# First head group's maxima rows, ones rows, two chunks of keys and first values made ready within the first pass over the context

## The chip, the cores and the metric

The kernel runs on one core of a Trainium2 chip as one program, in one launch. The metric is the time of one execution on the device, in microseconds (us). The profile adds the trace of one execution. Engines: TensorE (PE in the rows, its weight loads PEld), VectorE (DVE), ScalarE (ACT), GpSimd (POOL), and SyncE (SP), which issues the DMA transfers.

## The reference

A layer of a perceiver on 512 latents of 512 channels, with a context of 8192 rows. Only the first of its three parts is touched:

```python
def _L0_xattn_ref(query_modal, key_value_modal, Wq, bq, Wk, bk, Wv, bv, Wo, bo):
    q = _split_heads(query_modal @ Wq.T + bq)      # 16 heads of 32
    k = _split_heads(key_value_modal @ Wk.T + bk)
    v = _split_heads(key_value_modal @ Wv.T + bv)
    scores = jnp.einsum('bhnd,bhmd->bhnm', q, k) * scale
    attn = jax.nn.softmax(scores, axis=-1)
    x = jnp.einsum('bhnm,bhmd->bhnd', attn, v)
    ...
    return x @ Wo.T + bo

x = x + _L0_xattn_ref(_layernorm(x, axis=-1), ctx_1024, ...)
x = x + _L0_attn_ref(_layernorm(x, axis=-1), ...)   # self attention, then a sparse mixing over heads
x = x + _L0_ffn_ref(_layernorm(x, axis=-1), ...)    # 8 experts, top 2
```

## The kernel before

The program is a row of blocks. Each block holds a hand-written instruction list for every engine, ordered by semaphores, and no engine enters the next block before all have finished the one at hand.

**Preparation** (`prepare`, L113) makes the queries, and the keys of the first of 16 context chunks (512 rows each).

**First pass** (`project_context`, L278). It projects all chunks to keys and values and stores them in DRAM, since they don't fit in the on-chip memory, and finds for each query row and head the maximum score. `ITEMS` lists 32 projections (16 chunks for keys, 16 for values), each of four parts, numbered by `o`. GpSimd splits each chunk into a rounded high part (cast, L98) and the low rest (subtraction, L100), `split_chunk`. The maxima come from pairs of chunks: max(a, b) = (a + b)/2 + |a - b|/2, so keys are added and subtracted pairwise (`k_sum`, `k_dif`: on VectorE for the first pair, L502 and L503, on GpSimd later, L392 and L393). 256 steps (`STEPS`) follow, 32 for a pair of chunks (block `m`), eight for a head group `g` of four heads. In step `i` TensorE makes the difference scores of step i + 1 (`dif`, L430), once ScalarE has read those of step i (`s_size`, L445), the sum scores of step i (`tot`, two banks), and four or six matmuls of the projections (L86), into two banks `proj`. ScalarE takes the magnitude of the difference (L481) and evacuates finished projections (L470, L474). VectorE adds and takes the running maximum (L519). It may lag: TensorE's step i waits for the maxima of step i - 2 (L447). In the last block of chunks head group 0 is through at step 231, and `row_maxima` (L505) reduces the maxima of three head groups at step 248 and those of the last at the end.

SyncE stores keys and values (`store_keys`, L371). Behind the parts of the third-last and second-last items it also copies the queries into the tile `stacks` (`queries`, L356, twelve transfers a half). At the block's end it waits for all stores and copies (L376 to L381). TensorE ends with eight warm-up matmuls (`keep_warm`, L275).

**Second pass** (`attend_context`, L543). For each of four head groups it runs over all 16 chunks in tiles of 128 context rows, 64 tiles a group, numbered by `T`. Keys lie in one of three buffers `kst` with 98 rows: high keys, low keys, high keys again, and two rows of ones; values in one of three buffers `val`. One score matmul (L700) multiplies these with the tile `stacks`, whose 96 rows of queries are followed by two rows that hold the negated maximum, high and low part; so the scores come out shifted and ScalarE takes the exponential straight away (L801) into `pr`. TensorE weights the values (L714), VectorE adds up the exponentials (L851).

Before the first score matmul of this block, VectorE clears a tile and puts the negated maxima into it (L828 to L825), TensorE runs sixteen warm-up matmuls, transposes the tile (`turn`, L604), warms up again, ScalarE and VectorE copy the four rows into `stacks` (`take_row`, L610), GpSimd writes the ones rows of the three key buffers (L627, L631), ScalarE loads its table with a one-element exponential (L790), and SyncE loads keys (L656) and values (L661) of the first three chunks.

Of the kernel before, what the change touches and what calls it, by code (L numbers as in the profile page):

```python
# [20 lines left out]
P = 128  # L21
D = 512
# [255 lines left out]
def project_context(nc, c):  # L278
# [35 lines left out]
    with ExitStack() as stack:  # L314
# [12 lines left out]
        best = sb("best", [P, H * NT, BLOCKS])  # L327
        dif = pb("dif", [P, 2 * CH])
# [5 lines left out]
        v_out = [sem(f"v_out{w}") for w in range(2)]  # L334
        nc.clear_and_free_semaphores(c.spent)
        c.spent = used
        block = stack.enter_context(nc.Block())

# [6 lines left out]
        def _(sp):  # L345
# [12 lines left out]

            for o in range(4 * len(ITEMS)):
# [16 lines left out]
            for w in range(2):  # L376
                sp.wait_ge(k_hi_out[0][w], 16 * (NCH // 2))
                sp.wait_ge(k_hi_out[1][w], 16 * (NCH // 2))
                sp.wait_ge(k_lo_out[w], 16 * NCH)
                sp.wait_ge(v_out[w], 16 * NCH)  # L380
            sp.wait_ge(s_stack, 16 * 2 * 3 * HG)  # L381

        @block.gpsimd
        def _(pool):
# [9 lines left out]

            for i in range(2, len(ITEMS)):
                if i % 4 == 2 and i > 2:
                    pairs(i // 4)
                split_chunk(pool, c, i)

        @block.tensor  # L400
        def _(pe):
            def project(o, begin, end):
                kind, n = ITEMS[o // 4]
                b, at, out = o // 4 % RING, o % 4, proj[o % 2][:, :]
                if begin == 0:
                    if at == 0:
                        pe.wait_ge(c.s_lo, o // 4 + 1)

                    if kinds[o - 2] == "k":
# [27 lines left out]
            for i in range(STEPS):  # L437
# [13 lines left out]
                for piece in pieces(i):  # L451
                    project(*piece)
            pe.wait_ge(s_size, STEPS)
# [3 lines left out]
        def _(act):  # L457
# [19 lines left out]
            for i in range(STEPS):  # L477
# [4 lines left out]
                for o in finished(i):  # L482
                    evacuate(o)

        @block.vector
        def _(dve):
# [22 lines left out]

            LAST = STEPS - 2 * NT  # L510
            first_pair(0)
            low(FIRST - 1)
            for i in range(STEPS):
# [8 lines left out]
                for o in finished(i):  # L522
                    low(o)
                if i == LAST:
                    row_maxima(slice(0, HG * (G - 1)), LAST)
            row_maxima(slice(HG * (G - 1), H), STEPS)
            dve.wait_ge(s_best, 2)
# [15 lines left out]
def attend_context(nc, c):  # L543
# [26 lines left out]
    with ExitStack() as stack:  # L570
        sb, pb, sem = allocators(nc, stack, "att")
        kst = [sb(f"kst{b}", [STK + 2, HG, CH], F32R) for b in range(CHUNKS)]
        val = [sb(f"val{b}", [P, KT, P]) for b in range(CHUNKS)]
# [5 lines left out]
        k_in = [sem(f"k_in{b}") for b in range(CHUNKS)]  # L579
        v_in = [sem(f"v_in{b}") for b in range(CHUNKS)]  # L580
# [3 lines left out]
        s_row = [sem(f"row{half}") for half in range(2)]  # L584
# [25 lines left out]
        def take_row(engine, h, bank, done):  # L610

            j = h % HG
            src, dst = bank[HD * j:HD * j + 2, 0:N], c.stacks[MROW:MROW + 2, h, :]
            if engine.engine == mybir.EngineType.Activation:
                engine.activation(dst, src, ACT.Copy).then_inc(done, 1)
            else:
                engine.tensor_copy(dst, src).then_inc(done, 1)
# [1583 lines left out]
```

## Time and profile before

| | us |
|---|---|
| median of 3 runs | 1576.19 |
| lowest and highest run | 1572.24, 1576.27 |
| the profiled execution's time | 1577.37 |
| its span, first to last instruction | 1575.7 |

| engine | busy in the span |
|---|---|
| TensorE matmuls | 1506.9 us, 96% |
| VectorE | 1240.7 us, 79% |
| ScalarE | 1022.8 us, 65% |
| GpSimd | 410.5 us, 26% |

The busy share is a mean over stages with different limits, and it counts warm-up matmuls as work. Times within the trace run from the start of the span. The first pass lasts from about 47 to 570 us, the second from there to about 1140.

### The profile page before, as it was taken

Reading aid. Unit: us, or ns where it says so; the run is one execution under the profiler, and the core shown is the slowest. Engines: PE = TensorE matmul, PEld = TensorE weight load, DVE = VectorE, ACT = ScalarE, POOL = GpSimd, SP = SyncE. Lnnn points to the kernel's source line nnn. Section 1 sums busy time; section 2 is a strip of 40 time slices with the busy share of each in tenths; the row PEclk is TensorE's granted clock in tenths of the full one; section 3 lists DMA queues with packets and bytes.
Section 4 is the critical chain, followed back from the end, with each engine's and each line's share of the span. In section 5 each row is a group of like instructions: output and inputs, shape, how many; then the busy total and the mean of one; then the engine's idle time right before and its main releaser. Section 6 shows DMA issues by size and latency. Waiting matters only on the chain. (4 is left out here: it accounts for less than half of the span.)

```text
span 1575.7 us, 23638 instructions
## 1 busy us (share of the span) xinstructions
PE 1506.9 (96%) x8658; PEld 871.1 (55%) x8658; DVE 1240.7 (79%) x1876; ACT 1022.8 (65%) x1343; POOL 410.5 (26%) x225
## 2 busy tenths in 40 slices
PE   6899999999999999999999999999999955999998
PEld 4566666666666554444444444444345732799995
DVE  6777776776767769999998999999876878476664
ACT  3366666666666768888888888888737941244441
POOL 5554546545456010501200400100004420200002
PEclk9899999999999999999999999999999987899999
DMA  6354443544435365446645454445237045399994
GB/s 236 111 200 147 162 176 127 191 148 173 174 132 189 104 164 125 124 127 174 175 114 153 115 128 114 128 114 130 59 54 161 2 178 205 127 340 348 362 331 141
DMA packets 119778, 254.59 MB, mean 162 GB/s; under 512 B 10152, under 2 KB 26536, under 8 KB 115184
## 3 DMA queue, kind: packets, MB, share of 16 engines
q1 hardware_dynamic: 117632, 248.35, 50.6%
q0 software_dynamic: 1408, 4.46, 0.9%
q8 instruction: 70, 1.15, 0.3%
q10 hardware_dynamic: 624, 0.27, 0.1%
q14 instruction: 44, 0.36, 0.1%
HBM read 182.26 MB, written 61.34 MB: 155 GB/s over the span
## 5 line engine op out<-in xcount | busy, mean ns | idle before, releaser
L801 ACT ACTIVATE att_pr<-b_sc 128x1024 f32<-128x1024 f32 x512 | 482.2, 1035 | 74.8 <-PE b_sc L700 73.4
L851 DVE TENSOR_TENSOR att_tot<-att_tot,att_pr 128x2048 f32<-128x2048 f32 x184 | 430.2, 2338 | 21.4 <-ACT att_pr L801 3.3
L519 DVE CUSTOM_DVE_ANT_0 ctx_size<-ctx_tot,ctx_size 128x512 f32<-128x512 f32 x512 | 333.1, 689 | 130.5 <-PE ctx_tot L430 127.1
L481 ACT ACTIVATE ctx_size<-ctx_dif 128x1024 f32<-128x1024 f32 x256 | 262.4, 1025 | 122.6 <-PE ctx_dif L430 122.5
L700 PE MATMUL b_sc<-g_stacks,att_kst 98*128 98x512 f32 x1024 | 293.3, 418 | 2.0 <-DMA att_kst<-keys_scratch 1.5
L700 PEld LDWEIGHTS b_sc<-g_stacks,att_kst 98*128 98x128 f32 x1024 | 175.0, 188 | 186.1 <-ACT att_pr L801 136.2
L714 PE MATMUL b_o<-att_pr,att_val 128*32 128x512 f32 x2048 | 255.4, 600 | 0.9 <-issue 0.9
L430 PE MATMUL ctx_dif<-ctx_k_dif,f_q_hi 32*128 32x512 f32 x512 | 127.9, 497 | 7.3 <-DVE ctx_best L519 6.0
L430 PE MATMUL ctx_tot<-ctx_k_sum,f_q_hi 32*128 32x512 f32 x512 | 128.5, 499 | 0.0
L86 PE MATMUL f_proj<-g_stacks,f_wk_hi 128*128 128x512 f32 x352 | 120.4, 423 | 0.7 <-DVE f_k_lo L211 0.7
L86 PE MATMUL f_proj<-f_wv_hi,g_stacks 128*128 128x512 f32 x320 | 120.7, 421 | 0.0
L714 PEld LDWEIGHTS b_o<-att_pr,att_val 128*32 128x32 f32 x2048 | 48.8, 108 | 114.9 <-issue 95.2
L1907 PEld LDWEIGHTS ex_hp<-ex_xT,m_w 128*128 128x128 f32 x960 | 109.3, 192 | 3.0 <-issue 1.8
L1907 PE MATMUL ex_hp<-ex_xT,m_w 128*128 128x128 f32 x960 | 109.8, 275 | 0.8 <-issue 0.8
L430 PEld LDWEIGHTS ctx_dif<-ctx_k_dif,f_q_hi 32*128 32x128 f32 x512 | 47.6, 182 | 103.9 <-issue 52.4
L100 POOL TENSOR_TENSOR g_stacks<-f_raw,g_stacks 128x2048 fp32r<-128x2048 f32 x21 | 97.2, 4630 | 1.7
L1966 ACT ACTIVATE g_stacks<-m_w 128x1024 fp32r<-128x1024 f32 x56 | 54.6, 1047 | 63.9 <-PE ex_yp L86 63.9
L851 DVE TENSOR_TENSOR att_tot<-att_pr 128x2048 f32<-128x2048 f32 x36 | 84.1, 2335 | 13.0 <-ACT att_pr L801 13.0
L621 POOL TENSOR_TENSOR o_aoT<-att_whole,att_rs 128x512 f32<-128x512 f32 x3 | 9.4, 3141 | 324.2 <-DVE att_rs L858 324.2
L86 PEld LDWEIGHTS f_proj<-g_stacks,f_wk_hi 128*128 128x128 f32 x352 | 60.8, 191 | 30.0 <-issue 20.4
L86 PEld LDWEIGHTS f_proj<-f_wv_hi,g_stacks 128*128 128x128 f32 x320 | 59.6, 188 | 29.2 <-issue 18.3
L86 PE MATMUL f_proj<-f_wv_hi,f_third 128*128 128x512 f32 x192 | 72.4, 421 | 0.0
(314 smaller groups left out, 2182.2 us busy)
## 6 DMA issues: line engine op xcount, KB each, us to landing
m_w<-in_W SPq DMA_DIRECT2D x30, 2048.0 KB, 10.3
att_kst<-keys_scratch SPq DMA_DIRECT2D x192, 256.0 KB, 3.9
f_raw<-in_ctx SPq DMA_DIRECT2D x32, 1024.0 KB, 5.9
keys_scratch<-f_k_hi SPq DMA_DIRECT2D x32, 512.0 KB, 2.8
keys_scratch<-f_k_lo SPq DMA_DIRECT2D x32, 512.0 KB, 3.1
values_scratch<-ctx_v SPq DMA_DIRECT2D x32, 512.0 KB, 3.2
att_val<-values_scratch SPq DMA_DIRECT2D x64, 256.0 KB, 2.6
rows_scratch<-mix_blank SPq DMA_DIRECT2D x1, 3840.0 KB, 23.8
```

Of the source, the lines that this page charges most:

```text
L86: mm = pe.matmul(out, left, right, start=(n == 0), stop=(n == 3 * len(a) - 1))
L100: pool.tensor_tensor(c.lo[b], raw[:, :, :], f32(c.hi[b]), ALU.subtract).then_inc(c.s_lo, 1)
L430: mm = pe.matmul(out[:, r * CH:(r + 1) * CH], c.q_hi[rows, g, t * P:(t + 1) * P], keys[m % 2][rows, g, :], start=True, stop=True)
L481: act.activation(size[:, i % ABS, :], dif[:, :], ACT.Abs).then_inc(s_size, 1)
L519: dve.tensor_tensor_reduce(out=size[:, i % ABS, r * CH:(r + 1) * CH], in0=tot[i % 2][:, r * CH:(r + 1) * CH], in1=size[:, i % ABS, r * CH: ...
L621: engine.tensor_tensor(c.aoT[:, g, :], whole[:, :], rs[:, :], ALU.mult).then_inc(s_norm, 1)
L700: mm = pe.matmul(sc[pair % PAIRS][:, r * N:(r + 1) * N], kst[m % CHUNKS][:, j, at:at + P], c.stacks[0:STK + 2, HG * (T // PER_G) + j, :], ...
L714: mm = pe.matmul(o[at, :], val[m % CHUNKS][:, T % KT, at], pr[:, T % SLOTS, j, :], start=first, stop=False, skip_group_check=True)
L801: act.activation(pr[:, T % SLOTS, 2 * s:2 * s + 2, :], sc[(2 * T + s) % PAIRS][:, :].rearrange("p (j q) -> p j q", j=2), ACT.Exp, scale=SC ...
L851: dve.tensor_tensor(tot[b % 2][:, :, :], so_far, pr[:, T % SLOTS, :, :], ALU.add).then_inc(s_add, 1)
L1907: mm = pe.matmul(hp[tau % 2][:, f, :], w1[b][:, k, f * P:(f + 1) * P], xT[tau % 2][:, k, :], start=(k == 0), stop=(k == DC - 1))
L1966: act.activation(w2_hi[:, fs, :], w2[tau % 2][:, fs, :], ACT.Copy).then_inc(s_hid, 1)
```

## The change

Work that stood at the start of the second pass is done within the first, for head group 0 alone:

- Buffers: two of the key buffers `kst` and one of the value buffers are now allocated for both passes. They lie where the two buffers of raw context chunks (`raw`) lie, and later stages get their tiles at that place too (`same_place`).
- GpSimd clears a tile `first` at the start of the first pass, and at its end writes the ones rows of two key buffers.
- VectorE reduces the maxima of head group 0 at step `EARLY` = 232, and puts them into `first` at the next step (`first_shifts`).
- TensorE transposes `first` into a free bank `proj` at step `TURN` = 249, behind the matmuls of that step. Part 127, the last, uses the bank next and waits for the four row copies. ScalarE makes one copy in step 250 and two in step 251, VectorE one in step 251 (`take_row`).
- SyncE issues the keys of two chunks and the values of one (`first_keys`) right behind the query copies, ahead of the last two stores of values. The block's end waits for these loads and no longer for the last values: ScalarE and VectorE wait for those in the second pass, at its second tile and its start.
- ScalarE's one-element exponential stands at the end of the first pass.
- The second pass starts with the score matmuls. The warm-ups, the transposes and row copies ahead of them are gone.

```diff
+            def first_keys():
+                for w in range(2):
...
+                    sp.wait_ge(v_out[w], 16)
+                for b in range(2):
+                    sp.wait_ge(c.s_lo, len(ITEMS) - 1 + b)
+                    for row, part in ((0, 0), (1, 1), (2, 0)):
+                        sp.dma_start(f32(c.kst[b][HD * row:HD * row + HD, :, :]),
+                                     c.k_dram[b, 0, part].rearrange("(j d) k -> d j k", j=HG)).then_inc(c.k_first[b], 16)
+                sp.dma_start(c.val[:, :, :], c.v_dram[0, 0]).then_inc(c.v_first, 16)
...
                     queries(o // 4 - (len(ITEMS) - RING))
-            for w in range(2):
-                sp.wait_ge(k_hi_out[0][w], 16 * (NCH // 2))
...
-                sp.wait_ge(v_out[w], 16 * NCH)
+                    if o // 4 == len(ITEMS) - 2:
+                        first_keys()
             sp.wait_ge(s_stack, 16 * 2 * 3 * HG)
+            for b in range(2):
+                sp.wait_ge(c.k_first[b], 48)
+            sp.wait_ge(c.v_first, 16)
...
+            pool.memset(first[:, :, :], 0.0).then_inc(s_blank, 1)
             for i in range(2, len(ITEMS)):
...
+            for b in range(2):
+                pool.memset(f32(c.kst[b][MROW:MROW + 2, :, :]), 1.0).then_inc(s_ones, 1)
...
+                    if o == LATE + 2:
+                        pe.wait_ge(s_row, HG)
...
+                if i == TURN:
+                    pe.wait_ge(v_done, count("v", LATE + 1))
+                    pe.wait_ge(s_shift, 3)
+                    for tile in range(NT):
+                        mm = pe.transpose(turned[:, tile * P:(tile + 1) * P], first[:, tile, :], c.ident[:, :])
...
+                if i == TURN + 1:
+                    take_row(act, 0)
+                if i == TURN + 2:
+                    take_row(act, 1)
+                    take_row(act, 2)
+            act.activation(once[:, :], c.ones[:, 0:1], ACT.Exp).then_inc(s_once, 1)
...
+            def first_shifts():
+                parts = first[:, :, :].rearrange("p t (j w) -> p j t w", w=HD)
+                dve.wait_ge(s_best, 1)
+                dve.tensor_scalar(first_hi[:, :, :], c.neg[:, 0:HG, :], -1.0, None, ALU.mult).then_inc(s_shift, 1)
...
+                if i == EARLY:
+                    row_maxima(slice(0, HG), EARLY)
+                if i == EARLY + 1:
+                    first_shifts()
+                if i == TURN + 2:
+                    take_row(dve, HG - 1)
...
-            keep_warm(pe, den[:, 0:P], c.ident[:, :], c.ident[:, :], 16)
-            pe.wait_ge(s_shift, 4)
-            turn(pe, sc[0])
-            keep_warm(pe, den[:, 0:P], c.ident[:, :], c.ident[:, :], 4)
-            pe.wait_ge(s_ones, 1)
-            for half in range(2):
-                pe.wait_ge(s_row[half], HG // 2)
...
-            act.activation(std[:, 0:1], c.ones[:, 0:1], ACT.Exp).then_inc(s_early, 1)
-            act.wait_ge(s_turned, 1)
-            for h in range(1, HG, 2):
-                take_row(act, h, sc[0], s_row[1])
             for T in range(TILES):
...
+                elif T == 1:
+                    for w in range(2):
+                        act.wait_ge(c.v_out[w], 16 * NCH)
...
-            shifts(0)
-            dve.wait_ge(s_turned, 1)
-            for h in range(0, HG, 2):
-                take_row(dve, h, sc[0], s_row[0])
+            for w in range(2):
+                dve.wait_ge(c.v_out[w], 16 * NCH)
```

## Rows read from the trace of the kernel before

**Rows 1.** Busy us of each engine by stretch; then granted clock, DMA share, GB/s.

```profile
700.00:800.00 100.00, 100.00 (x608) 42.61 (x610) 95.59 (x45) 86.29 (x93) 16.84 (x6) 1.00 0.62 165
```

**Rows 2.** Groups of TensorE in the second pass: busy, mean ns | idle before, releasers.

```profile
L700 PE MATMUL b_sc<-g_stacks,att_kst 98*128 98x512 f32 x1024 | 293.3, 418 | 2.0 <-DMA att_kst<-keys_scratch 1.5 <-ACT att_pr L801 0.5
```

**Rows 3.** Timeline between the passes: start us, duration us, engine, line [idle before <-releaser].

```profile
566.59 2.14 PE L275 MATMUL ctx_dif<-f_wv_hi 128*128 128x512 f32 x8
...
568.16 0.29 DVE L507 TENSOR_REDUCE g_neg<-ctx_best 128x16 f32<-128x128 f32 x1
570.42 1.80 POOL L627 MEMSET att_kst<- 2x2048 f32 x1 [54.99 <-POOLq L314]
570.42 1.28 ACT L790 ACT_TABLE_LOAD   x1 [3.56 <-PEq L314]
570.42 1.28 SPq L656 DMA_DIRECT2D att_kst<-keys_scratch  x3
...
570.46 3.81 PE L275 MATMUL b_den<-g_ident 128*128 128x128 f32 x32 [1.73 <-PEq L314]
...
571.00 1.27 DVE L829 TENSOR_SCALAR att_shift_hi<-g_neg 128x64 fp32r<-128x64 f32 x1
...
572.30 0.18 DVE L824 COPY o_yT<-att_shift_hi 128x16 f32<-128x16 f32 x1
...
574.10 0.60 PE L607 MATMUL b_sc<-g_ident,o_yT 128*128 128x128 f32 x4
...
574.74 1.20 ACT L615 ACTIVATE g_stacks<-b_sc 2x512 fp32r<-2x512 f32 x2 [2.82 <-PE b_sc L607]
...
577.08 1.63 PE L700 MATMUL b_sc<-g_stacks,att_kst 98*128 98x512 f32 x6 [1.49 <-DMA att_kst<-keys_scratch]
```

**Rows 4.** SyncE's waits in 540 to 600 us: total, times, longest.

```profile
SPq L380 <- DMA values_scratch<-ctx_v: 2.4, 1, 2.4
```

**Rows 5.** Stretches by engine as in rows 1, opening and boundary.

```profile
60.00:62.00 2.00, 2.00 (x9) 1.07 (x8) 2.00 (x6) 0.25 (x1) 1.72 (x1) 0.50 0.00 0
74.00:78.00 4.00, 4.00 (x15) 2.29 (x12) 2.47 (x7) 1.77 (x3) 0.00 (x0) 0.50 0.02 4
560.00:562.00 2.00, 2.00 (x13) 1.07 (x10) 1.44 (x6) 1.62 (x3) 0.00 (x0) 1.00 0.00 0
572.00:574.00 2.00, 2.00 (x21) 2.00 (x20) 0.53 (x3) 0.00 (x0) 0.21 (x1) 1.00 0.99 246
```

**Rows 6.** Timeline of the first pass's opening.

```profile
47.05 0.70 PE L86 MATMUL f_proj<-f_third,f_wk_hi 128*128 128x512 f32 x2 [0.30 <-PEq L117]
47.32 2.18 POOL L98 CAST g_stacks<-f_raw 128x2048 fp32r<-128x2048 f32 x1 [15.14 <-POOLq L117]
...
47.66 2.38 DVE L503 TENSOR_TENSOR ctx_k_sum<-f_k_hi 128x512 fp32r<-128x512 f32 x1
...
58.69 0.50 PE L430 MATMUL ctx_dif<-ctx_k_dif,f_q_hi 32*128 32x512 f32 x2 [2.84 <-DVE ctx_best L519]
...
62.20 0.68 DVE L503 TENSOR_TENSOR ctx_k_sum<-f_k_hi 128x512 fp32r<-128x512 f32 x1
...
66.81 4.74 DVE L502 TENSOR_TENSOR ctx_k_dif<-f_k_hi 128x512 fp32r<-128x512 f32 x1
```

**Rows 7.** Timeline of SyncE's issues near the first pass's end.

```profile
554.01 2.52 SPq L356 DMA_DIRECT2D g_stacks<-g_hT  x4
557.16 10.10 SPq L371 DMA_DIRECT2D values_scratch<-ctx_v  x2
```

**Rows 8.** Timeline of the first pass's last steps.

```profile
556.79 0.55 DVE L507 TENSOR_REDUCE g_neg<-ctx_best 128x48 f32<-128x384 f32 x1
...
558.12 0.18 PEld L430 LDWEIGHTS ctx_dif<-ctx_k_dif,f_q_hi 32*128 32x128 f32 x2 [0.42 <-ACT ctx_size L481]
...
558.66 1.03 ACT L481 ACTIVATE ctx_size<-ctx_dif 128x1024 f32<-128x1024 f32 x1 [0.60 <-PE ctx_dif L430]
558.81 0.69 DVE L519 CUSTOM_DVE_ANT_0 ctx_size<-ctx_tot,ctx_size 128x512 f32<-128x512 f32 x1 [0.25 <-PE ctx_tot L430]
```

More of the change, by code:

```diff
@@ L333, in project_context @@
         k_hi_out, k_lo_out, s_pair0 = c.k_hi_out, c.k_lo_out, sem("pair0")
-        v_out = [sem(f"v_out{w}") for w in range(2)]
+        v_out = c.v_out = [sem(f"v_out{w}") for w in range(2)]
+        c.k_first, c.v_first = [sem(f"k_first{b}") for b in range(2)], sem("v_first")
+        s_ones, s_blank, s_shift, s_turned, s_row, s_once = (
+            sem(n) for n in ("ones", "blank", "shift", "turned", "row", "once"))
         nc.clear_and_free_semaphores(c.spent)
@@ L583, in attend_context @@
         s_rs, s_norm, s_out = sem("rs"), sem("norm"), sem("out")
-        s_row = [sem(f"row{half}") for half in range(2)]
+        s_row = sem("row")
         shift_hi = sb("shift_hi", [P, H, NT], F32R)
@@ L612, in take_row @@
             j = h % HG
[L613 to L617, printed above, removed]
+            engine.tensor_copy(c.stacks[MROW:MROW + 2, h, :], bank[HD * j:HD * j + 2, 0:N]).then_inc(done, 1)
         def weigh(engine, g):
@@ L654, in _ @@
                     sp.wait_ge(s_sc, 2 * KT * (m - CHUNKS + 1))
-                for row, part in ((0, 0), (1, 1), (2, 0)):
+                for row, part in ((0, 0), (1, 1), (2, 0)) if m >= len(c.kst) else ():
                     sp.dma_start(f32(kst[b][HD * row:HD * row + HD, :, :]),
@@ L977, in self_projections @@
         rstd = sb("rstd", [P, 2, H])
[L978 removed]
+        cen = c.cen
         sq = sb("sq", [P, D])
@@ L2096, in perceiver_layer, with same_place @@
         c.stacks = sb("stacks", [P, H, N], F32R)
+        def same_place(*shapes):
+            with ExitStack() as room:
+                sb, _, _ = allocators(nc, room, "k")
+                return [sb(name, shape, dt) for name, shape, dt in shapes]
+        c.raw = same_place(*((f"raw{b}", [P, DC, CH], F32) for b in range(2)))
+        (c.cen,) = same_place(("cen", [P, 3, D], F32))
+        c.held, c.wide, c.room = same_place(*((n, [P, 2, N], F32) for n in ("held", "wide", "room")))
+        c.z, c.left, c.zs = same_place(*((n, [P, 2, N], F32) for n in ("z", "left", "zs")))
+        c.hid_hi, c.hid_lo = ([tile[:, FC * b:FC * b + FC, :] for b in range(2)] for tile in same_place(
+            *((n, [P, 2 * FC, P], F32R) for n in ("hid_hi", "hid_lo"))))
+        c.kst = [sb(f"kst{b}", [P, HG, CH], F32R) for b in range(2)]
+        c.val = sb("val", [P, KT, P])
         with ExitStack() as first:
```

93 lines of the change are left out of this document (57 added, 36 removed).

## The prediction

> **What bounds the kernel now.** I read the busy time by stretch first. In 700 to 800 us, inside the second pass over the context, TensorE is busy all 100 us at full granted clock, VectorE 95.6, ScalarE 86.3 [rows 1]. The list of groups for the whole second pass says the same: before all 1024 score matmuls TensorE sat idle 2.0 us, of which 1.5 us waited for a key load [rows 2]. So the pass cannot be shortened by this change, but it can start earlier, and what is taken off before its first score matmul moves everything behind it by as much, because no stage between there and the end starts by an outside event.
>
> Then I read the timeline between the passes [rows 3]. The last work of the first pass is TensorE's eight warm-up matmuls, ended by 566.59 + 2.14 = 568.73, and VectorE's last maximum, ended by 568.45. All engines set off again only near 570.4. Then: shifts on VectorE, four transposes on TensorE at 574.10, row copies from 574.74, and the first score matmul at 577.08, released by a key load that was issued at 570.42. From 568.73 to 577.08 are 8.35 us in which TensorE does nothing that the result needs, save the transposes. The list of the queue's waits names what held the block's end: SyncE waited 2.4 us for the last store of values [rows 4]. Key loads of the second pass cannot be issued sooner, as they stand behind that end. In 572 to 574 us the DMA engines are 0.99 busy, in 560 to 562 they move nothing [rows 5].
>
> **What is removed.** Before the first scores: the warm-up and transposes on TensorE (3.81 + 0.60 us and another small warm-up), the table load (1.28), the row copies (1.20 for ScalarE's two), the first wait for keys, and SyncE's 2.4 us wait, since the block's end no longer asks for the last values. What then ends the first pass is TensorE's warm-up and VectorE's maximum. At the boundary before, from preparation to first pass, where no store was awaited, TensorE sat idle 0.30 us [rows 6]. So without any added cost the first score matmul would start at 568.73 + 0.30 = 569.03, which is 8.05 us earlier.
>
> **What is added, and where it shows.**
>
> *The blank tile's memset, on GpSimd at the start of the first pass.* GpSimd's memset of 2048 elements per partition took 1.80 us [rows 3]; 512 elements make some 0.45 us by that row. There GpSimd is on the path: its cast and subtraction of a chunk share time with VectorE's sums of the first keys. A sum took 2.38 us while the cast ran and 0.68 us when it didn't, and TensorE then waited 2.84 us for VectorE [rows 6]. So I count the whole 0.45 us. From below it is 0 (something else later); from above 0.45 + 0.68 = 1.13, if a sum of VectorE also gets in ahead of the delayed cast.
>
> Of this the Trainium skill (SBUF — State Buffer, "Who interferes with whom") says that a VectorE instruction with two SBUF inputs is held by a GpSimd instruction that reads SBUF, not by one that only writes it, and that whichever starts first holds the other. The cast and the 2.38 us agree. By that rule the memset would not hold the sum at 47.66, which would run before the cast; the cast would end 0.7 us later, the subtraction behind it would be spared the sum that now delays it by 0.3, and the cost would be 0.4 instead of 0.45.
>
> *Seven loads of 256 KB on SyncE's queue (six of keys, one of values), ahead of the last two stores of values.* SyncE issues the second half of the query copies until 556.5, then stands waiting; its next store was issued at 557.16 [rows 7]. Seven issues at 0.43 us (three took 1.28 [rows 3]) are 3.0 us, so that store moves to about 559.6, and nobody waits for it until the second tile of the second pass. The data is 1.84 MB, with the store 2.36 MB; at the 246 GB/s of 572 to 574 [rows 5] this takes 9.6 us from 556.5, so it lands near 566, in a stretch that is now empty. The block's end at about 570 waits for it, so the cover is some 4 us; it is gone when the rate falls under 172 GB/s (2.36 MB in 13.7 us). I take 0. The last store has landed today when the block ends, near 570.4, and with 1.5 us of later work (below) near 571.9. ScalarE's second tile, which now waits for it, comes behind two exponentials, each as large as the magnitude that took 1.03 us [rows 8], so not before 570.5 + 2.06 = 572.6. So 0 again, with 0.7 us to spare.
>
> *The ones rows on GpSimd (two of 1.80 us).* They follow its last chunk split; GpSimd was idle 54.99 us before the second pass [rows 3]. 0.
>
> *First maxima, and three small operations on VectorE, some 23 steps before the end.* A step lasts 1.03 + 0.60 = 1.63 us, ScalarE's magnitude and its wait; VectorE sits idle 0.25 in it [rows 8]. A reduction three times as long as the new one took 0.55 and did no harm. Small operations took 0.18; 1.27 is the longest such row, beside a running GpSimd memset [rows 3]. TensorE's step waits for the maxima of two steps before, so a short lag of VectorE reaches nobody. I take 0; from above 0.8 us, if one lasts 1.27.
>
> *Four transposes on TensorE, three row copies on ScalarE, one on VectorE, in the last seven steps.* This is the term that counts. ScalarE and TensorE hand each step to one another: ScalarE is free 0.60 us of a step, TensorE 0.42 [rows 8]. Transposes took 0.60 [rows 3], so the next step's difference starts some 0.2 late. The first copy (0.60) waits for them and starts late by as much again: ScalarE's next magnitude is 0.45 later than now. The two other copies stand in one step: 1.20 us in a gap of 0.60, so 0.60 more. Together 1.05. From below 0.6 (only the second of the pair shows), from above 1.8 (three copies with no gap at all). VectorE's copy ends 0.69 + 2 × 0.69 + 0.60 = 2.67 us into its step (start of its maxima, the two, a copy as long as ScalarE's), TensorE wants it for the last projection after 1.63 + 0.60 = 2.23: 0.44 late, which the 0.42 us gap swallows. I take 0, from above 0.45.
>
> *The exponential's table on ScalarE at the end.* 1.28 us and one tiny operation, 0.2 at most, behind the last values. ScalarE has ended today 3.56 us before 570.42 [rows 3]; with 1.5 us of later work and this it ends at 569.85, TensorE's warm-up at 570.23. 0, with only 0.4 us of cover.
>
> The remaining edits only give tiles other places, or move shifts within VectorE, which has nothing to add until two exponentials are done. 0.
>
> **Sum.** First scores at 569.03 + 0.45 + 1.05 = 570.53 instead of 577.08: 6.55 us gained. With all lower costs 569.63 (7.45 gained), with all upper ones 569.03 + 1.13 + 0.8 + 1.8 + 0.45 = 573.21 (3.87 gained). The profiled execution took 1577.37 for a span of 1575.7, so the span becomes 1569.2 and that execution 1570.8. It lies 1.2 us above the median of the runs, 1576.19; from that median the forecast is 1569.6.
>
> **Rivals.**
>
> *The boundary still waits for a transfer (8%).* The loads go out behind twelve query copies, and today's first key load took 6.6 us to release TensorE, sharing the engines with the other loads [rows 3, 5]. For: that figure. Against: the empty stretch. If they land at 572.5 to 575 the gain is 2 to 4.5 us, 1571.7 to 1574.2. TensorE would then idle longer; in 60 to 62 us, after its 2.84 us wait, its granted clock was 0.50, that is 1.2 GHz instead of 2.4, while the idle 1.73 us at today's boundary left it at 1.00 [rows 3, 5, 6].
>
> Beside this stands the Trainium skill (TensorE: Matmul & The Clock Gate, "Part 1"): idleness of the array throttles its clock to half, sustained work restores it. The trace agrees at 60 to 62 us. The warm-ups that the change takes out would matter by that rule only if the idle time between the passes grew, and here it falls to 0.3.
>
> *The added work costs its upper bounds (12%).* Terms next to 1.13 and 1.8, with a second loss in the opening: 2 to 4.5 us gained, again 1571.7 to 1574.2. For: 0.60 us gaps are already full in steps with an evacuation. Against: copies are spread over two steps.
>
> *Slower, by a new collision in the opening (6%).* Four pairs of VectorE's sums meet GpSimd's chunk splits; the worst of them took 4.74 instead of 0.68 us, the one at 62.20 ran free [rows 6]. If the delayed GpSimd catches that pair too, with its subtraction and the cast behind it, the two sums cost 4.06 + (2.38 - 0.68) = 5.76 more. Behind such a wait the granted clock was 0.50 through 74 to 78 us [rows 5], 2 us lost of these 4: 7.76 in all, net 1.2 us slower, 1577.4. It decides from the point where new collisions cost over 6.55. Against: GpSimd would have to come some 4 us later against VectorE than now, and it comes 0.45 later.
>
> **Chances and range.** The forecast has 74%: 3.9 to 7.5 us by its bounds, mostly over 5.5. About 0.3%, 4.7 us, is what a measurement of this kernel can tell from no change. Faster by more than that: 0.78 (the forecast and the better edge of the first two rivals); within it 0.16; slower 0.06. The runs before spread over 4 us, so the range goes from 1565.5 (7.45 gained and three more by the runs) to 1573.5, which takes in the better part of both rivals.
>
> **What would show it.** Right: first scores about 6.5 us earlier, TensorE idle under 0.5 us at the boundary, no key wait, and the second pass and all behind it as long as before. The steps with the row copies 1 us longer together, the opening 0.4. Wrong: TensorE waiting for a load or for SyncE at the boundary, more than 2 us lost in the last seven steps, or VectorE's sums in the opening waiting longer than now.

## The result, and the profile after

The changed kernel takes 1567.71 us (median of 9 runs, 1563.96 to 1568.89), the kernel before, run beside it, 1575.34 (9 runs, 1570.35 to 1576.39). The ratio is 0.9947, with a 95% interval of 0.9934 to 0.9961; as a share of 1575.34 us that is 8.35 us less, between 6.1 and 10.4. The forecast was 1569.6, and 6.55 us less. The profiled execution took 1565.9 us for a span of 1564.2.

The timeline between the passes answers to [rows 3]:

```profile
567.07 2.12 PE L275 MATMUL ctx_dif<-f_wv_hi 128*128 128x512 f32 x8
...
567.37 1.28 ACT L535 ACT_TABLE_LOAD   x1
...
568.64 0.29 DVE L561 TENSOR_REDUCE g_neg<-ctx_best 128x16 f32<-128x128 f32 x1
...
569.50 1.63 PE L760 MATMUL b_sc<-g_stacks,g_kst 98*128 98x512 f32 x6 [0.30 <-PEq L314]
```

From the start of the closing warm-up to the first score matmul it is 569.50 - 567.07 = 2.43 us, where it was 577.08 - 566.59 = 10.49 [rows 3]. TensorE stands idle 0.30 us, as long as at the other boundary [rows 6]. No load or store is awaited between the passes any more. These are all of SyncE's waits in 540 to 600 us, with total, times and longest (before: [rows 4]); none is for a store or a load:

```profile
SPq L404 <- ACT ctx_v L520: 17.7, 2, 9.3
SPq L729 <- PE b_o L774: 11.4, 3, 4.1
SPq L720 <- PE b_sc L760: 8.3, 3, 3.9
SPq L314 <- PEq L314: 1.3, 1, 1.3
```

SyncE's issues (before: [rows 7]) and the DMA's mean rate through the same stretch, in GB/s for each of 40 slices of 553 to 572 us, 0.475 us each:

```profile
552.49 2.52 SPq L375 DMA_DIRECT2D g_stacks<-g_hT  x4
555.35 2.72 SPq L388 DMA_DIRECT2D g_kst<-keys_scratch  x6
558.11 0.43 SPq L390 DMA_DIRECT2D g_val<-values_scratch  x1
558.59 9.15 SPq L404 DMA_DIRECT2D values_scratch<-ctx_v  x2
```

```profile
GB/s 190 198 211 224 207 194 203 112 220 319 207 194 203 267 250 246 263 207 207 203 254 246 211 242 373 386 336 43 0 0 0 0 274 345 345 140 34 172 371 367
```

The six key loads and the load of values leave between 555.35 and 558.54. The engines then move data without a pause until slice 28, that is up to 553 + 28 × 0.475 = 566.3 us, and nothing for the four slices behind it: the loads have landed some 3 us before the passes meet. What moves from 568.2 us on begins with the last store of values, for which nobody waits there. The last seven steps of the first pass (before: [rows 8]) hold the transposes and the row copies:

```profile
556.30 1.02 ACT L527 ACTIVATE ctx_size<-ctx_dif 128x1024 f32<-128x1024 f32 x1
...
557.22 0.60 PE L497 MATMUL f_proj<-g_ident,ctx_first 128*128 128x128 f32 x4
...
557.85 0.58 ACT L354 ACTIVATE g_stacks<-f_proj 2x512 fp32r<-2x512 f32 x1 [0.53 <-PE f_proj L497]
...
558.46 1.02 ACT L527 ACTIVATE ctx_size<-ctx_dif 128x1024 f32<-128x1024 f32 x1
...
559.51 1.20 ACT L354 ACTIVATE g_stacks<-f_proj 2x512 fp32r<-2x512 f32 x2
...
560.74 1.02 ACT L527 ACTIVATE ctx_size<-ctx_dif 128x1024 f32<-128x1024 f32 x1
...
561.58 0.70 DVE L356 CAST g_stacks<-f_proj 2x512 fp32r<-2x512 f32 x1
```

ScalarE's magnitudes start 2.16 us apart over the first copy (556.30 to 558.46) and 2.28 over the pair (558.46 to 560.74), where 1.62 is the rule. And the opening of the first pass (before: [rows 6]):

```profile
48.90 0.52 POOL L428 MEMSET ctx_first<- 128x512 f32 x1 [17.00 <-POOLq L117]
...
49.25 0.68 DVE L557 TENSOR_TENSOR ctx_k_sum<-f_k_hi 128x512 fp32r<-128x512 f32 x1
49.37 2.32 POOL L98 CAST g_stacks<-k_raw 128x2048 fp32r<-128x2048 f32 x1
...
68.64 4.74 DVE L556 TENSOR_TENSOR ctx_k_dif<-f_k_hi 128x512 fp32r<-128x512 f32 x1
```

The second pass itself is as full as it was; the stretch of 700 to 800 us answers to [rows 1], the group of score matmuls to [rows 2]:

```profile
700.00:800.00 100.00, 100.00 (x611) 42.14 (x611) 96.78 (x45) 86.78 (x93) 16.84 (x6) 1.00 0.61 163
```

```profile
L760 PE MATMUL b_sc<-g_stacks,g_kst 98*128 98x512 f32 x688 | 201.5, 419 | 0.9 <-ACT att_pr L860 0.6
...
L760 PE MATMUL b_sc<-g_stacks,att_kst 98*128 98x512 f32 x336 | 94.7, 412 | 0.0
```

Of the 1.5 us that the score matmuls waited for a key load [rows 2] nothing is left.

The two spans differ by 11.5 us, more than the runs do. I measured the same stretches in every trace of this study, from the starts of fixed instructions:

| trace | last seven steps | boundary | first to last exponential | experts |
|---|---|---|---|---|
| before | 11.35 | 10.49 | 554.05 | 215.00 |
| control (before once more) | 11.35 | 11.31 | 555.04 | 215.02 |
| before_again | 11.35 | 11.06 | 556.14 | 215.02 |
| swap_before | 11.35 | 10.43 | 556.19 | 214.36 |
| places | 11.34 | 11.32 | 553.58 | 213.42 |
| keys_only | 11.35 | 8.16 | 553.61 | 213.42 |
| rows_only | 12.58 | 9.24 | 554.14 | 213.47 |
| store_wait | 12.57 | 3.79 | 553.56 | 213.48 |
| store_again (the same) | 12.57 | 3.80 | 555.39 | 213.47 |
| after | 12.57 | 2.42 | 553.57 | 213.48 |
| after_again | 12.58 | 2.42 | 553.68 | 213.46 |
| swap | 12.54 | 2.44 | 553.52 | 213.47 |
| late_turn | 11.94 | 2.97 | 553.60 | 213.47 |
| best | 11.95 | 2.96 | 553.58 | 213.58 |

"Last seven steps" runs from ScalarE's magnitude of step 248 to that of step 255, "boundary" from the warm-up's start to the first score matmul, "experts" from the expert stage's first matmul to the end. Most of what is left of the 11.5 us lies in stretches that move without any change: the first pass from step 11 to 221 took 426.2 us in before and control and 424.8 in before_again, the same kernel, and 421.3 and 424.8 in store_wait and store_again, again one kernel.

### The profile page after: what moved, and what is told of

Its sections match the earlier page's. It is cut to its first block and busy times, and to the rows that moved or that the text cites. A ratio compares the mean times of both kernels' runs of the same rounds, so it can differ in the third digit from the quotient of the medians.

```text
span 1564.2 us, 23569 instructions
## 1 busy us (share of the span) xinstructions
PE 1498.1 (96%) x8618; PEld 865.7 (55%) x8618; DVE 1236.9 (79%) x1877; ACT 1023.1 (65%) x1344; POOL 410.4 (26%) x226
## 5 line engine op out<-in xcount | busy, mean ns | idle before, releaser
L760 PE MATMUL b_sc<-g_stacks,g_kst 98*128 98x512 f32 x688 | 201.5, 419 | 0.9 <-ACT att_pr L860 0.6
L760 PEld LDWEIGHTS b_sc<-g_stacks,g_kst 98*128 98x128 f32 x688 | 116.0, 188 | 137.1 <-ACT att_pr L860 98.4
L774 PE MATMUL b_o<-att_pr,att_val 128*32 128x512 f32 x1344 | 166.4, 600 | 0.9 <-issue 0.9
L100 POOL TENSOR_TENSOR g_stacks<-k_raw,g_stacks 128x2048 fp32r<-128x2048 f32 x21 | 97.0, 4618 | 1.7
L760 PE MATMUL b_sc<-g_stacks,att_kst 98*128 98x512 f32 x336 | 94.7, 412 | 0.0
L774 PE MATMUL b_o<-att_pr,g_val 128*32 128x512 f32 x704 | 89.1, 601 | 0.0
L760 PEld LDWEIGHTS b_sc<-g_stacks,att_kst 98*128 98x128 f32 x336 | 59.0, 188 | 48.2 <-ACT att_pr L860 37.9
## 6 DMA issues: line engine op xcount, KB each, us to landing
m_w<-in_W SPq DMA_DIRECT2D x30, 2048.0 KB, 10.4
```

The source lines that it names most:

```text
L100: pool.tensor_tensor(c.lo[b], raw[:, :, :], f32(c.hi[b]), ALU.subtract).then_inc(c.s_lo, 1)
L760: mm = pe.matmul(sc[pair % PAIRS][:, r * N:(r + 1) * N], kst[m % CHUNKS][:, j, at:at + P], c.stacks[0:STK + 2, HG * (T // PER_G) + j, :], ...
L774: mm = pe.matmul(o[at, :], val[m % CHUNKS][:, T % KT, at], pr[:, T % SLOTS, j, :], start=first, stop=False, skip_group_check=True)
```

## The experiments

**control.** The kernel before, unchanged, as a measure of the measurement.

> The kernel before, unchanged, as a second profile of it. Call B the stretch from the eight warm-up matmuls that end the first pass to the first score matmul of the second: 10.49 us in the kernel before, 2.43 in the changed one. If the gain is all in B, B is 10.5 here again and the ratio 1.000. The changed kernel's trace also had a first pass 1.1 us shorter and later stages some 4 us shorter than the trace of before. If that is chance from one execution to another, this second trace of the same kernel differs from the first by as much in those stages; if it comes from the change, this trace agrees with the first within 0.5 us there.

1575.77 us (12 runs), ratio 1.0009 [0.9997, 1.0022]: no difference, as it should be. Its boundary was 11.31 us, so the boundary alone moves by some 0.8 from one execution to the next. Its experts took 215.02 us as before, so the 1.5 us that the changed kernel gains there are not scatter.

**keys_only.** From the kernel before: the shared buffers, the early loads, the early ones rows and the later wait for the last values; the maxima, their transposes and the row copies stay in the second pass.

```diff
+                    if o // 4 == len(ITEMS) - 2:
+                        first_keys()
-                sp.wait_ge(v_out[w], 16 * NCH)
+            for b in range(2):
+                sp.wait_ge(c.k_first[b], 48)
+            sp.wait_ge(c.v_first, 16)
```

> Keys, values and ones rows early, and no wait for the last values at the end of the block; the maxima rows are made at the start of the second pass as before, with the warm-ups. Theory (what is removed are two chains side by side, the key load and the making of rows, and only taking both away starts the scores): the chain of rows is left, 5.8 us from the release of the boundary to the end of the row copies, so B is 2.4 + 5.8 = 8.2 and the time some 2.3 us under before, 0.9985. Rival (the key load was the wait, as the list of waits names it in front of the first score matmul, and early loads alone bring the gain): B 2.5 to 4, the time 6 to 8 us under before, 0.995 to 0.996.

Boundary 8.16 us; 1568.03 us (12 runs), ratio 0.9964 [0.9949, 0.9979]. The timeline shows the chain that is left when no load is awaited:

```profile
568.33 3.81 PE L275 MATMUL b_den<-g_ident 128*128 128x128 f32 x32 [0.30 <-PEq L314]
...
571.98 0.60 PE L627 MATMUL b_sc<-g_ident,o_yT 128*128 128x128 f32 x4
...
572.61 1.41 DVE L637 CAST g_stacks<-b_sc 2x512 fp32r<-2x512 f32 x2 [3.32 <-PE b_sc L627]
...
574.07 1.66 PE L721 MATMUL b_sc<-g_stacks,g_kst 98*128 98x512 f32 x6 [0.60 <-DVE g_stacks L637]
```

The warm-up begins 0.30 us after the block, and the scores wait for VectorE's copies. The boundary came out as expected, and the rival's 2.5 to 4 us did not. The time is lower than I expected, close to what the rival gave: this kernel has the new tile places too, with which the experiment `places` deals.

**rows_only.** From the changed kernel: SyncE loads keys and values in the second pass again, and the block's end waits for the stores of all keys and of the first chunk's values.

```diff
-                    if o // 4 == len(ITEMS) - 2:
-                        first_keys()
+                sp.wait_ge(v_out[w], 16)
...
-                for row, part in ((0, 0), (1, 1), (2, 0)) if m >= len(c.kst) else ():
+                for row, part in ((0, 0), (1, 1), (2, 0)):
```

> The maxima rows made early as in the changed kernel, no wait for the last values, but the keys and values of the first chunks loaded at the start of the second pass. Theory: the first key load is left, 6.6 us from its issue at the release to the first score matmul, so B is 2.4 + 6.6 = 9.0; against 1.5 us gained there stand 1.65 us of added work in the first pass, so the time is that of before, 0.999 to 1.001. Rival (the making of the rows was the wait, the load would have landed earlier without the traffic of three chunks): B 4 to 6, 0.996 to 0.9975.

Boundary 9.24 us; 1572.72 us (12 runs), ratio 0.9991 [0.9977, 1.0005].

```profile
568.92 1.28 SPq L706 DMA_DIRECT2D g_kst<-keys_scratch  x3
...
575.76 1.65 PE L745 MATMUL b_sc<-g_stacks,g_kst 98*128 98x512 f32 x3 [7.10 <-DMA g_kst<-keys_scratch]
```

With the rows ready, TensorE waits 7.10 us for the first keys, which were issued at 568.92. So the row chain and the load stood side by side in the kernel before, each nearly as long as the boundary: taking away either alone saves 2 to 3 of the 8 to 9 us (11.31 - 8.16 and 11.31 - 9.24 in the same series of runs; against the shortest old boundary of the table, 10.43, it is 2.3 and 1.2). Both kernels also drop the wait for the last values, and that brings TensorE's first instruction of the second pass forward by 1.43 us (2.42 us behind the start of the closing warm-up in keys_only, 3.85 in control). What either chain saves by itself is less by as much.

**store_wait.** The changed kernel, whose block's end waits for the last values again.

```diff
             sp.wait_ge(c.v_first, 16)
+            for w in range(2):
+                sp.wait_ge(v_out[w], 16 * NCH)
```

> The changed kernel with one wait put back: the block of the first pass ends only when the last values are stored. Theory: the last store is issued some 0.3 us after the warm-up matmuls begin and lands 3.0 us later, so B is 3.5 instead of 2.43 and the time 1.1 us over the changed kernel, 0.9955 of before against 0.9947. Rival (the wait hides behind the table load, the last maxima and the warm-up): B stays 2.4, no difference.

Boundary 3.79 us, 1.37 more than with the change; 1569.52 us (13 runs), ratio 0.9965 [0.9950, 0.9979].

```profile
558.74 2.12 PE L275 MATMUL ctx_dif<-f_wv_hi 128*128 128x512 f32 x8
...
562.53 1.61 PE L762 MATMUL b_sc<-g_stacks,g_kst 98*128 98x512 f32 x6 [1.67 <-PEq L314]
```

```profile
SPq L416 <- DMA values_scratch<-ctx_v: 2.5, 1, 2.5
```

SyncE's wait is 2.5 us, close to the 2.4 of [rows 4], but only 1.37 of it shows; the rest falls within the closing warm-up. This trace is not a typical one: its execution took 1557.32 us, the other twelve 1565.97 to 1572.49. Its boundary is confirmed by store_again.

**places.** The kernel before with nothing but the new allocation: shared `kst` and `val` where `raw` lies, and later stages' tiles at that place (`same_place`).

```diff
+        c.raw = same_place(*((f"raw{b}", [P, DC, CH], F32) for b in range(2)))
+        c.z, c.left, c.zs = same_place(*((n, [P, 2, N], F32) for n in ("z", "left", "zs")))
...
+        c.kst = [sb(f"kst{b}", [P, HG, CH], F32R) for b in range(2)]
+        c.val = sb("val", [P, KT, P])
...
-            c.raw = [sb(f"raw{b}", [P, DC, CH]) for b in range(2)]
...
-        hid_hi = [sb(f"hid_hi{b}", [P, FC, P], F32R) for b in range(2)]
-        hid_lo = [sb(f"hid_lo{b}", [P, FC, P], F32R) for b in range(2)]
+        hid_hi, hid_lo = c.hid_hi, c.hid_lo
```

> The kernel before with the changed kernel's places for its tiles (shared key, value and raw buffers, all tiles behind them shifted, hidden tiles of the experts at the shared place), and nothing moved in time. In the first three traces of kernels with those places the wide steps of the first pass (12 to 222) took 424.8 us against 426.2 in both traces with the old ones, the experts to the end 213.45 against 215.0, and the exponentials of the second pass 553.6 against 554.05 and 555.04. Theory (a matmul's pitch depends on where its operands lie): the same 424.8, 213.5 and 553.6 here, B 10.5 as before, and the time some 3.4 us under before, 0.9978. Rival (the moved work or the earlier start does it): 426.2, 215.0, and 1.000.

1572.81 us (12 runs), ratio 0.9982 [0.9968, 0.9997]. The boundary is that of before, but the experts take 213.42 us instead of 215.02. The answers for the expert stage's output tile show where: duration in ns (shortest, median, longest) of two of its three groups of 512-column products, first in the kernel before, then in places.

```profile
L86 PE MATMUL ex_yp<-g_stacks,ex_hid_hi x112: 393/394/482, 1378.8 to 1555.2; 128*128 128x512 f32 x112
L86 PE MATMUL ex_yp<-m_w_lo,ex_hid_hi x112: 393/394/398, 1379.1 to 1555.4; 128*128 128x512 f32 x112
```

```profile
L86 PE MATMUL ex_yp<-g_stacks,k_hid_hi x112: 388/390/477, 1378.2 to 1553.0; 128*128 128x512 f32 x112
L86 PE MATMUL ex_yp<-m_w_lo,k_hid_hi x112: 386/390/397, 1378.5 to 1553.3; 128*128 128x512 f32 x112
```

394 ns became 390. From the start of a product with the low weights to the start of the next it was 233 ns (median) in the three traces with the old places and 227 in those with the new ones. 336 products at 4 to 6 ns make 1.3 to 2.0 us, and 1.6 are measured. The second pass gains too: from its 32nd exponential to its last the four traces with the old `kst` and `val` (swap_before is one) take 0.42 to 0.49 us longer than the changed kernel, places and the other traces with the new ones at most 0.08.

**swap and swap_before.** Which tile does it? `swap` is the changed kernel with the hidden tiles `hid_hi` and `hid_lo` at a place of their own and the low weights `w2_lo` at the shared one. `swap_before` makes the same exchange in the kernel before.

```diff
-        c.hid_hi, c.hid_lo = (... same_place(... "hid_hi", "hid_lo"))
+        (c.w2_lo,) = same_place(("w2_lo", [P, FC, D], F32R))
...
-                c.w2_lo = sb("w2_lo", [P, FC, D], F32R)
+                c.hid_hi, c.hid_lo = (... sb(n, [P, 2 * FC, P], F32R) for n in ("hid_hi", "hid_lo"))
```

> The changed kernel with two tiles of the experts exchanged: the low part of the second weights lies at the shared place, and the high and low hidden tiles where it lay. Theory A (the place of the hidden tiles, which are the stationary operand of these products, decides): the experts to the end take 215.0 us again. Theory B (the place of the low weights, moving operand, decides): 213.5 or less. Nothing else changes; the time is within 1.6 us of the changed kernel, 0.9947 to 0.9957.

> The kernel before with two tiles of the experts exchanged: hidden tiles, high and low, where the low part of the second weights lay, and that where they lay. Theory (the place of the hidden tiles, the stationary operand, decides the pitch of these products): experts to the end 213.5 instead of 215.0. Rival (something else of the new places, or of the program, decides): 215.0. The rest as in the kernel before, the ratio 0.999 or 1.000.

`swap`: experts 213.47 us; 1564.08 us (6 runs), ratio 0.9919 [0.9905, 0.9933]. `swap_before`: experts 214.36; 1575.04 us (10 runs), ratio 0.9987 [0.9975, 1.0000]. So moving the hidden tiles away from the shared place doesn't undo the gain, and the exchange gives 0.66 us of it to the kernel before. In `swap_before` the shortest products are as short as in places, the median as long as before:

```profile
L86 PE MATMUL ex_yp<-g_stacks,m_hid_hi x112: 387/394/478, 1377.2 to 1553.0; 128*128 128x512 f32 x112
L86 PE MATMUL ex_yp<-ex_w_lo,m_hid_hi x112: 388/396/398, 1377.6 to 1553.2; 128*128 128x512 f32 x112
```

That the places of the tiles decide the time of these products is shown; which operand's, and by what property of its address, is not. Theory A of `swap` fails (213.47 us, not 215.0), which does not yet show theory B; in `swap_before` neither the 213.5 of the theory nor the 215.0 of the rival came, but less than half of the gain.

**late_turn.** The changed kernel with the turn one part later (`LATE` + 1, so `TURN` = 250) and one copy of ScalarE's in each of three steps. No projection uses the bank again, so TensorE's wait for the copies falls away.

```diff
-        LATE = 4 * len(ITEMS) - 3
+        LATE = 4 * len(ITEMS) - 2
...
-                    if o == LATE + 2:
-                        pe.wait_ge(s_row, HG)
...
                     take_row(act, 1)
+                if i == TURN + 3:
                     take_row(act, 2)
```

> The changed kernel with the transposes one part later, in the bank that no later part needs: row copies of ScalarE in the last three steps, one in each, VectorE's in the last but one, and no wait of the last part for them. Steps 249 to 256 took 11.35 us before and 12.57 with the change. Theory (the loss there is the pair of copies in one step, 0.6, and the late start behind the transposes, the rest): 11.8 here, B up to 0.3 us longer than 2.42, since the table load comes after one more copy; in all 0.5 us under the changed kernel. Rival (the copies cost the same wherever they stand): 12.5.

Last seven steps 11.94 us: of the 1.22 that the copies cost, 0.63 is won. But the boundary is 2.97, 0.55 longer, and the time of 1568.03 us (6 runs), ratio 0.9946 [0.9932, 0.9961], is that of the changed kernel.

```profile
564.84 2.14 PE L275 MATMUL ctx_dif<-f_wv_hi 128*128 128x512 f32 x8
564.90 0.70 DVE L356 CAST g_stacks<-f_proj 2x512 fp32r<-2x512 f32 x1
...
566.24 0.69 DVE L584 CUSTOM_DVE_ANT_0 ctx_size<-ctx_tot,ctx_size 128x512 f32<-128x512 f32 x1
...
566.97 0.29 DVE L560 TENSOR_REDUCE g_neg<-ctx_best 128x16 f32<-128x128 f32 x1
...
567.81 1.62 PE L759 MATMUL b_sc<-g_stacks,g_kst 98*128 98x512 f32 x6 [0.84 <-PEq L314]
```

VectorE's row copy now stands among its last maxima. VectorE ends at 567.26, 0.28 behind TensorE's warm-up (566.98), where it ended ahead of it with the change (568.93 against 569.19). ScalarE ends at 567.24, 0.02 ahead of VectorE. TensorE idles 0.84 us instead of 0.30; the experiment `best` tells the two engines apart.

**best.** late_turn, with the memset moved behind the last chunk split and the table load to the start of the first pass, to take it from the boundary.

```diff
-            pool.memset(first[:, :, :], 0.0).then_inc(s_blank, 1)
             for i in range(2, len(ITEMS)):
...
+            pool.memset(first[:, :, :], 0.0).then_inc(s_blank, 1)
...
+            act.activation(once[:, :], c.ones[:, 0:1], ACT.Exp).then_inc(s_once, 1)
             evacuate(FIRST - 1)
```

> late_turn, with two more edits: the memset of the blank tile stands behind GpSimd's last chunk split, and the one-element exponential with its table load at the start of the first pass, where ScalarE is idle. Theory: steps 249 to 256 11.8 us, B 2.42 or somewhat less, the opening 0.4 us shorter (which its scatter between executions, 28.4 to 32.7 us, hides; so read there whether the first cast starts with the block); in all 1.2 us under the changed kernel, 0.994 of before. Rival (a table with the exponential doesn't serve the first pass and is loaded again): a second table load in the first pass or at its end, 1.3 us.

Boundary 2.96 us, so my expectation for it fell: it was not the table load that made it longer, as without it the boundary is the same. The rival is out as well: the trace has no second load of this table in the first pass. With ScalarE out of question, VectorE remains as what ends last, with its copy in the place shown for late_turn; that the copy alone makes the 0.55 us is read from the order of the rows, not tested by moving it. 1564.73 us (6 runs), ratio 0.9925 [0.9911, 0.9939]. That interval meets the changed kernel's; that of swap, [0.9905, 0.9933], ends just below it, though no stretch of its trace in the table shows a gain. The three kernels late_turn, best and swap, run on one chip, spread by 4 us while those stretches agree within 0.6. I don't call any of them better than the change, and where swap's lower time comes from is open.

**before_again, after_again, store_again.** The kernel before, the changed kernel and store_wait, each profiled once more, to tell what belongs to the kernel and what to one execution.

> The kernel before once more, for a third trace. Two stretches differ between the traces so far: experts to the end 215.0 us (both traces with old places) against 213.4 to 213.6 (all eight with new ones), wide steps 32 to 222 of the first pass 385.7 (both old, and one of the new) against 384.4 (six of the new) and 381.3 (one). If the places decide, 215.0 and 385.7 here; if the level is drawn at each execution, others can come.

> The changed kernel once more. If the places decide both stretches, 213.5 and 384.4; if the level of the first pass is drawn at each execution, 384.4 need not come again. B 2.42 and steps 249 to 256 12.57 in any case.

> The changed kernel with the wait for the last values put back, once more: its first trace had 381.3 us in steps 32 to 222, with the same TensorE program as the changed kernel. If the build decides this level, 381.3 again; if the execution, most likely 384.4. B 3.8 in any case.

1576.86, 1566.28 and 1571.41 us. Experts, last steps and, for the changed kernel and store_wait, the boundary came back within 0.02 us. The first pass from step 11 to 221 took 424.8 us in before_again, with the old places, and 426.2 in best, with the new ones: unlike the experts, it isn't decided by the places, as the theory of `places` had it. The start of the second pass did not come back: in before_again and store_again the first 32 exponentials take 2.1 and 1.7 us longer than with the change, and in the view by stretches the column behind the busy times, the granted clock, is the difference that goes with it. First before_again, then store_again, then the changed kernel's second trace, the first 8 to 12 us of the second pass:

```profile
576.00:580.00 4.00, 3.81 (x13) 1.82 (x12) 0.27 (x1) 4.00 (x5) 1.29 (x1) 0.63 1.08 237
580.00:584.00 4.00, 4.00 (x14) 1.97 (x14) 4.00 (x4) 2.42 (x3) 0.00 (x0) 0.51 0.53 122
584.00:588.00 4.00, 4.00 (x28) 1.62 (x30) 2.71 (x2) 2.97 (x5) 0.00 (x0) 1.00 0.79 190
```

```profile
572.00:576.00 4.00, 4.00 (x11) 2.38 (x12) 1.68 (x2) 3.29 (x4) 1.74 (x1) 0.65 0.70 189
576.00:580.00 4.00, 4.00 (x13) 1.49 (x13) 3.38 (x4) 2.42 (x4) 0.00 (x0) 0.50 0.58 143
```

```profile
569.00:573.00 4.00, 3.44 (x12) 1.88 (x12) 1.68 (x2) 3.29 (x4) 1.73 (x1) 1.00 0.61 178
573.00:577.00 4.00, 4.00 (x28) 1.45 (x30) 3.39 (x4) 4.00 (x6) 0.00 (x0) 1.00 0.77 211
```

In before_again and store_again TensorE is granted 0.50, that is 1.2 GHz instead of 2.4, for 6.8 us, before it is back at 1.00. The timelines, of before_again and then of store_again, tell what it did before:

```profile
567.99 3.81 PE L275 MATMUL b_den<-g_ident 128*128 128x128 f32 x32 [1.76 <-PEq L314]
...
575.18 1.63 PE L700 MATMUL b_sc<-g_stacks,att_kst 98*128 98x512 f32 x6 [2.05 <-DMA att_kst<-keys_scratch]
```

```profile
568.18 2.11 PE L275 MATMUL ctx_dif<-f_wv_hi 128*128 128x512 f32 x8
571.98 4.86 PE L762 MATMUL b_sc<-g_stacks,g_kst 98*128 98x512 f32 x12 [1.69 <-PEq L314]
```

In before_again it had been idle for 1.76 and 2.05 us, in store_again for 1.69.

## Why the prediction was right, step by step

**The boundary: 8.05 us forecast, 8.06 measured** (10.49 - 2.43). The step stands as written: 0.30 us of idleness, nothing awaited. That the two numbers agree to 0.01 is luck, as the old boundary lies between 10.43 and 11.32 us in five traces. What the forecast did not say, keys_only and rows_only show: the 8 us are not a sum of parts. Each of the two chains filled most of the boundary alone, and the store's wait came ahead of both. With that wait dropped too, the early loads alone give 3.2 us and the early rows alone 2.1; putting the wait back into the changed kernel costs 1.37.

**The loads: forecast 0, right.** They landed 3 us ahead of the need, where 4 were forecast. Their transfer was slower than estimated: from the end of the query copies (552.49 + 2.52 = 555.01) to the silence at 566.3 are 11.3 us, and 9.6 were forecast. That the date near 566 comes out all the same is luck: in this trace the copies ended 1.5 us earlier than before [rows 7]. The rival of a boundary that waits for a transfer is out: no line of SyncE's waits, and 0.30 us of TensorE.

**Transposes and row copies: 1.05 us forecast, 1.22 measured,** in the same two steps and for the reason given: 0.45 + 0.60 were forecast, 2.16 - 1.62 = 0.54 and 2.28 - 1.62 = 0.66 were read. rows_only shows the same 1.23 without the early loads. The wait for the transposes was in the forecast, but a little too short: they ended at 557.82, only 0.10 us before the next magnitude was due (556.30 + 1.62 = 557.92), so the first copy of 0.58 cost almost its whole length. The rival of upper costs, 1.8 us here, is out. VectorE's copy, taken at 0, did hold TensorE for 0.32 us in front of its last projection; ScalarE's next magnitude came 0.03 late.

**The memset: 0.45 us forecast, 0.16 to 0.29 measured.** The instruction took 0.52 us. Its effect on the opening can't be read from one trace, as the stretch from step 0 to 11 takes 28.4 to 32.7 us, with half clock at other times in each, and in store_wait not at all. Between traces whose granted clock ran alike it is 0.16 (before and after_again, 32.26 and 32.42) and 0.26 to 0.29 (late_turn 31.35, against 31.09 in best and places and 31.06 in keys_only, which have no memset there). VectorE's sum at 49.25 took 0.68 us though the memset ran until 49.42, and now began ahead of the cast.

That the sum was not held is what the Trainium skill (SBUF — State Buffer, "Who interferes with whom") gives for a GpSimd instruction that only writes; the trace agrees, with 0.68 us against the 2.38 that the sum took beside the cast.

The cast behind it took 2.32 us (2.18 before), and the subtraction that follows 4.55 where it had taken 4.89: part of the delay came back there.

The rival of a new collision in the opening is out: the worst sum of before, 4.74 us, is 4.74 again, and no other joined it; the largest growth of another is that of the difference behind the sum named above, from 3.48 us in before to 3.73.

**The other terms taken at 0** stayed there. The stretch with the first maxima, step 221 to 248, took 44.66 us in before and 44.63 with the change; the first 32 exponentials, among them the tile that now waits for the last values, 32.77 and 32.75. ScalarE ended with its table at 568.86, 0.33 us ahead of TensorE's warm-up, where a cover of 0.4 was forecast.

**The term that was mis-sized: "The remaining edits only give tiles other places ... 0".** It is worth 1.55 us in the expert stage, 215.0 against 213.4 to 213.6, in all ten traces with the new places and in none of the three of the kernel before. places alone makes the kernel faster, with a ratio of 0.9982 [0.9968, 0.9997]. Another 0.4 to 0.5 us lies in the second pass, as shown under places. I had looked at these edits for the work that they issue, which is none, and not at the matmuls that read from there.

**What the forecast left out.** It was made against a trace in which the second pass began at full clock. In control, before_again and swap_before, all with the old boundary, it began with a stretch at half clock, and the first 32 exponentials took 1.1 to 2.2 us longer than in the changed kernel; in rows_only, with a boundary of 9.24, 0.6, in store_again 1.7. In before, store_wait and keys_only the granted clock stayed at 1.00 and they took no longer. In places they took no longer either, though the clock fell there too:

```profile
577.00:581.00 4.00, 4.00 (x11) 2.98 (x12) 0.00 (x0) 3.20 (x4) 1.78 (x2) 0.57 1.07 234
```

The price goes with how far the half clock reached into the pass, counted from the first score matmul: 3.8 us in places at no cost, 5.9 in rows_only for 0.6, 6.8 in control for 1.1, 8.0 in store_again for 1.7, 8.7 in before_again for 2.1 and 8.9 in swap_before for 2.2. In the five traces with a boundary under 3 us the granted clock stays at 1.00 through these 12 us.

Of this the Trainium skill (TensorE: Matmul & The Clock Gate, "Part 1") says that an idle array falls to half clock, and that the number of matmuls which run at half clock when a kernel starts varies from run to run. The traces agree that the fall follows idle time, and go further at this boundary: whether it comes at all varies, as store_wait idled 1.67 us without it and store_again, the same program, 1.69 with it.

**Sum.** 8.06 - 1.22 - 0.2 + 1.55 + 0.4 = 8.6 us, and up to 2 more where the old boundary cost the clock. The runs give 8.35, between 6.1 and 10.4, an interval that holds the 6.55 of the forecast too; so it is the traces that put the gain some 2 us above the forecast, and the term that makes it so in them is that of the places.

## What to carry to other kernels

At a boundary where several chains stand side by side, add up what is left when all of them are gone, and expect little from any part alone; then look which engine ends last, since late_turn won 0.63 us in the steps and gave 0.55 back when VectorE became the last one. A change of buffers is not free of effect because it issues nothing: list the matmuls that read the moved tiles. And read one trace against a second one of the same kernel before a stretch of it is put down to the change.

## What the runs showed of the hardware

The spacing of products of 512 columns, from the start of one to the start of the next, differed at the same granted clock of 1.00. In the experts it went with the places of the tiles (a median of 233 ns in the three traces with the old ones, 227 in the ten with the new ones). In the first pass it went with the execution: in the trace of store_wait the projections stood most often 227 ns apart (median 229), in store_again, the same program, 231 or 236 (median 233), and the pass took 3.5 us more (421.3 and 424.8 us for steps 11 to 221). No run here tells why. The same trace of store_wait is the only one whose clock did not fall in the opening either: it stood at 1.00 from 16 to 1190 us, where each of the other thirteen traces shows 0.50 at least twice before 80 us.

Idle times of 1.4 to 2.3 us ahead of the scores were followed by half clock in some executions and not in others: with 1.74 and 1.44 us in swap_before, but not with 1.73 and 1.49 in before. The price was up to 2.2 us (swap_before).
